# Moving VectorE's and ScalarE's side work around the exponentials in a two-layer kernel on one Trainium2 core

## What is computed

```python
h = gelu(einsum('bnd,hd->bnh', x, fc1_w) + fc1_b)            # 2048 hidden features
shared = einsum('bnh,sh->bns', h, fc2_w) + fc2_b             # 384 features
expert_x = einsum('bnh,bph->bnp', h, experts_w[indices]) + experts_b[indices][:, None, :]
x = x + concatenate([shared, expert_x], -1)
attn_in = tanh(einsum('bsd,da->bsa', x, W1) + b1)
scores = einsum('bsa,a->bs', attn_in, v)
mask = where(pt == 0, l <= j, where(pt == 1, l >= j, l != j))
p = softmax(where(mask, scores[:, None, :], -1e30), -1)
x = x + einsum('bjl,bld->bjd', p, x) / cnt[..., None]
```

## Time and profile before

| | us |
|---|---|
| time, median of 3 runs (1546.91 to 1548.66) | 1547.05 |
| the profiled execution's own time | 1547.54 |
| its span, first to last instruction | 1545.8 |
| TensorE busy | 1448.0 (94%) |
| VectorE busy | 1194.9 (77%) |
| ScalarE busy | 671.7 (43%) |
| mean granted TensorE clock | 0.974 of full speed |

### The profile page before, as it was taken

The page is one execution under the profiler, slowest core; times in us unless marked ns, Lnnn a source line. Parts: engine busy times, 40 slices in busy tenths (PEclk is TensorE's granted clock), DMA queues, the critical chain, the costliest instruction groups (busy, mean ns, idle before and its releaser), DMA issues.

```text
span 1545.8 us, 16174 instructions
## 1 busy us (share of the span) xinstructions
PE 1448.0 (94%) x6488; PEld 663.3 (43%) x6488; DVE 1194.9 (77%) x1749; ACT 671.7 (43%) x889; POOL 0.2 (0%) x4
## 2 busy tenths in 40 slices
PE   6999898999989999899998989999899998989986
PEld 2444343444434444344443434444344443434444
DVE  6867959688595876958689596886958779596885
ACT  4737154361723527145261633517245271542612
POOL 0000000000000000000000000000000000000000
PEclk9999999999999999999999999999999999999998
DMA  5220010201102020010200102010020200100000
GB/s 198 89 82 1 21 62 8 75 1 45 37 14 68 1 80 3 21 62 7 75 1 21 62 14 69 1 55 28 14 68 1 82 0 21 62 7 21 1 28 27
DMA packets 27149, 59.25 MB, mean 38 GB/s; under 512 B 5699, under 2 KB 6083, under 8 KB 24643
## 3 DMA queue, kind: packets, MB, share of 16 engines
q1 hardware_dynamic: 26642, 57.70, 10.8%
q10 hardware_dynamic: 432, 0.53, 0.1%
HBM read 41.45 MB, written 16.78 MB: 38 GB/s over the span
## 4 chain that ended last, share of the span: by engine, by line
PE 58%; DVE 33%; ACT 7%; issue 1%; DVEq 0%
PE pf L279 29%; PE po L325 24%; DVE raw L147 8%; DVE raw L381 7%; DVE hl L153 4%; PE pa L356 4%; DVE xr L147 3%; DVE raw L431 3%; ACT raw L414 3%; DVE mx L197 2%; DVE x L197 2%; ACT L414 1%; ACT hh L156 1%; PE pf L366 1%; ACT g L303 1%
## 5 line engine op out<-in xcount | busy, mean ns | idle before, releaser
L279 PE MATMUL pf<-xh,w1h 128*128 128x512 f16 x1024 | 389.7, 381 | 3.1 <-ACT xh L156 2.1
L279 PE MATMUL pf<-xh,w1l 128*128 128x512 f16 x1024 | 389.1, 380 | 0.4 <-DVE w1l L153 0.4
L279 PE MATMUL pf<-xl,w1h 128*128 128x512 f16 x1024 | 389.2, 380 | 0.1
L325 PE MATMUL po<-hh,w2l 128*128 128x512 f16 x768 | 301.8, 393 | 16.4 <-DVE hl L153 16.4
L325 PE MATMUL po<-hh,w2h 128*128 128x512 f16 x768 | 299.7, 390 | 0.0
L325 PE MATMUL po<-hl,w2h 128*128 128x512 f16 x768 | 299.0, 389 | 0.0
L153 DVE SCALAR_TENSOR_TENSOR hl<-g,ix,hh 128x512 f16<-128x512 f32 x240 | 177.6, 740 | 142.5 <-ACT hh L156 142.0
L303 ACT ACTIVATE g<-pf,b1s,ds 128x512 f32<-128x512 f32 x240 | 185.7, 774 | 148.9 <-PE pf L279 148.7
L381 DVE TENSOR_TENSOR_SCAN raw<-raw 128x512 f32<-128x512 f32 x180 | 212.9, 1211 | 47.6 <-ACT raw L414 47.6
L147 DVE TENSOR_TENSOR raw<-raw 128x512 f32<-128x512 f32 (+1 forms) x315 | 206.5, 683 | 1.0
L156 ACT ACTIVATE hh<-g,ix 128x512 f16<-128x512 f32 x240 | 173.1, 721 | 7.4
(11 more groups left out here) (121 smaller groups left out, 1195.1 us busy)
## 6 DMA issues: line engine op xcount, KB each, us to landing
er<-in_ew SPq DMA_DIRECT2D x16, 1024.0 KB, 4.8
out<-xr SPq DMA_DIRECT2D x64, 256.0 KB, 2.3
xr<-in_xT SPq DMA_DIRECT2D x62, 256.0 KB, 4.1
raw<-in_w SPq DMA_DIRECT2D x16, 256.0 KB, 6.5
er<-in_w SPq DMA_DIRECT2D x3, 1024.0 KB, 10.0
xr<-in_xT ACTq DMA_DIRECT2D x2, 256.0 KB, 5.1
raw<-in_aw SPq DMA_DIRECT2D x1, 256.0 KB, 6.3
ebs<-in_eb SPq DMA_DIRECT2D x16, 0.5 KB, 2.1
```

The costliest lines, as they stand in the source:

```text
L279: return e.matmul(pf[n][:, :], w[:, k, c, :], x[:, c, :], start=c == 0 and i == 0, stop=c == KD - 1 and i == 2)
L325: m = e.matmul(bank[:, :], w, h[:, k, :], start=k == 0 and i == 0, stop=k == NH - 1 and i == 2)
```

## The change

Nothing is computed in another way. TensorE's queue is the same, instruction for instruction. What moves:

- `exps` goes from k = 10 to k = 9, with `finish` before it, and `pool_rest` starts at k = 12.
- `x_biggest(b + 1)` goes from k = 13 to k = 9, the maximum of er from k = 14 to k = 10.
- `split_expert(b, j)` goes from k = 6 to 9 to the second layer's o = 0, one quarter in each j.
- In rows 1 to 14 the four `split_x_high` of the next row go from (0, 3), where they stood together behind `chain_scale`, to (1, 2), (1, 3), (2, 0) and (2, 2), so behind `evacuate(b, 0)`.
- In the last row the four `see` go from k = 10 to 13 to k = 0 to 3, and one of their work tiles takes the other half of er.
- The budgets are 1.75 for each k (1.1 at k = 1), the guessed costs count times 0.92, and the quarters that split the expert count 0.7 of their budget as spent.

```diff
-            credit[0] -= cost * 0.9
+            credit[0] -= cost * 0.92
...
-    same = er[:, 0, 0:S]
+    same = er[:, 1, 0:S]
...
-            if 6 <= k < 10:
-                split_expert(b, k - 6)
-            if k == 13 and not last:
-                x_big = x_biggest(b + 1)
-            if k == 14 and not last:
-                e_big = column(ec(b + 1), er[:, b % 2, :], e_ready[b + 1])
-            if last and 10 <= k < 14:
-                see(b, k - 10)
-            if k == 10:
+            if last and k < 4:
+                see(b, k)
+            if k == 9:
                 finish()
                 exps(b - 1)
+            if k == 9 and not last:
+                x_big = x_biggest(b + 1)
+            if k == 10 and not last:
+                e_big = column(ec(b + 1), er[:, b % 2, :], e_ready[b + 1])
+            if k == 12:
                 pools[0] = pool_rest(b - 1)
-            fill(0.0 if k in (13, 14) else 1.1 if 6 <= k < 10 else 1.85)
+            fill({1: 1.1}.get(k, 1.75))
...
                 if b == 0:
                     first_second_layer(o, j)
+                elif o == 0:
+                    split_expert(b, j)
+                    spent += 0.7
...
-                        x_hi = {c: split_x_high(b + 1, c) for c in range(KD)}
+                        if b == 0:
+                            x_hi = {c: split_x_high(1, c) for c in range(KD)}
                         spent += 0.6
+                    if b and (o, j) in ((1, 2), (1, 3), (2, 0), (2, 2)):
+                        c = ((1, 2), (1, 3), (2, 0), (2, 2)).index((o, j))
+                        x_hi[c] = split_x_high(b + 1, c)
```

## The result

| | kernel before | changed kernel |
|---|---|---|
| median of runs | 1547.86 us (4 runs, 1546.91 to 1549.01) | 1443.26 us (4 runs, 1443.10 to 1443.96) |
| ratio, 95% interval | | 0.9325, 0.9309 to 0.9341 |
| profiled execution, its span | 1547.54, 1545.8 | 1443.96, 1442.1 |

A forecast was written before the change was run, and what follows sets the result against it. TensorE waits for hl and x2l (1.23 + 3.48 us a round) and then runs at low clock (2.2). 96.2 from fourteen rounds, plus 8.0, less 1.4, is 102.8 off the span: 1444.2 us forecast, range 1441 to 1459.

The forecast's parts named there:

- The round without waits: Score to next score in rows 1 to 14 without waits or low clock: 86.6 us, against a mean of 93.47.
- the meeting: TensorE's attention product at output tile 0 and VectorE's x2l arrive within a tenth; 0.1 us of waiting per round taken.
- the walk-through: The change followed instruction by instruction on batch row 8's old clock, putting x2l at 823.3 and the attention product at 823.92.
- two queues at once: Why x2l is late: ScalarE evacuates po0 behind four xh, and VectorE works without a gap; mending one leaves the other.
- The maxima under the exponentials: VectorE's maxima of x and er cost the path nothing while it waits for exponentials; without that cover, 4.85 us.
- The clock: TensorE's low clock behind the long x2l wait, on average 2.2 us a round, goes with the wait.
- Rival B: Small TensorE waits lower the clock too, so 14 x 2.2 = 31 us come back: 1475; chance 0.03.
- The last row: Last batch row's transposes came 6.0 us late, plus 2.2 of clock; new residual about 0.2 late: gain 8.0.
- A: x2l misses TensorE's attention product by 0.5 to 1 us per round: 1450 to 1457; chance 0.09.
- C: Expert's weights land too late for their earlier maximum on VectorE, making it slower: 1561 at 1 us more; chance 0.01.
- D: Something other than these queues holds x2l: 1529 if only the hl wait goes, 1547 if it returns; chance 0.02.
- next in line: Tile 1's attention product could start at 833.9, TensorE there at 835.1; first-layer tile 14's banks keep as much room.

The follow-up runs named there:

- three products: Changed kernel plus three chained, unused 128x512 VectorE operations ahead of the residual of output tile 0: 1474.87 us, ratio 0.9524.
- five products: Changed kernel plus five chained, unused 128x512 VectorE operations ahead of the residual of output tile 0: 1515.43 us, ratio 0.9785.

## Why the prediction was right, point by point

**The sum.** Forecast were 96.2 us from the rounds less 1.4 of remaining waits, and 8.0 from the last row: 102.8 of span. Measured, from the scores of both traces:

| stretch | before | after | gain | forecast |
|---|---|---|---|---|
| to the first score | 117.63 | 118.56 | -0.93 | 0 |
| fourteen rounds | 1308.58 | 1212.53 | 96.05 | 94.8 |
| last row, up to its score | 90.16 | 82.59 | 7.57 | 8.0 |
| behind it | 29.43 | 28.42 | 1.01 | 0 |
| span | 1545.8 | 1442.1 | 103.7 | 102.8 |

The round without waits, 52.70 + 33.87 = 86.57, was right to 0.04. It was taken from one round of before by subtracting two waits and one stretch of low clock, and that is what is left when they are gone. Its halves were less good, and part of the hit is luck: with x2l early (expert's split back) the attention product starts 52.49 behind the score and not 52.70, and from there to the next score it is 34.1 and not 33.87. The first error comes from the due time, which gave the last product ahead of the attention product a whole interval of 0.217, where with x2l early the attention product starts 0.03 behind it (776.32 and 776.35). The low clock's 2.92 were too many by about as much: 865.49 - 828.70 - 34.1 = 2.7. The 1.4 for the meeting were caution: the profile has no wait there, and x2l holds the product by some 0.05 us.

**The meeting.** Scores stood at 771.29 before and 724.79 after, so 46.50 more puts a time of after on the clock of the walk-through:

| | forecast | measured |
|---|---|---|
| maximum of er starts | 790.9 | 744.36 + 46.50 = 790.86 |
| idle time of VectorE before hl of tile 10 | 3.7 | 3.67 |
| hl of tile 11 starts | 798.2 | 751.73 + 46.50 = 798.23 |
| hl of tile 15 starts | 809.6 | 763.01 + 46.50 = 809.51 |
| hl of tile 11 to x2l | 25.10, less 0.12 | 776.60 - 751.73 = 24.87 |
| x2l starts | 823.2 | 776.60 + 46.50 = 823.10 |
| attention product starts | 823.92, due 823.99 | 777.34 + 46.50 = 823.84 |

The sum of some 40 instruction lengths, each from a row of before, missed by 0.1 us. The added products show what that accuracy was needed for: the room is 0.03 us. 0.1 us later, and each round would have been longer by 0.07. The forecast couldn't know this room: x2l came 0.1 earlier than it had and TensorE's own due time was 0.2 earlier, both more than 0.03. That the two errors left no more between them is luck; 0.1 us more would have been 14 x 0.1 = 1.4 in all.

**ScalarE.** The evacuation came 6.8 us ahead of the residual where I had 6. That the xh and VectorE's queue had to be mended together was argued from rows and is now shown from both sides: the xh alone give nothing, and without them 6.7 us of the gain are lost. The first half is shown more sharply than the argument had it. I had called it two queues late at once; VectorE alone held x2l: po0 was evacuated at 824.07 + 0.72 = 824.79, and VectorE came to it at 825.67. None of the 3.32 us of wait came from ScalarE, so the sentence "two queues at once" was wrong, and the one behind it, that mending one alone would leave the other, holds very unequally: mending ScalarE's alone gave nothing, mending VectorE's alone gave all but 6.7 us. ScalarE's queue would have become the limit after the first 0.9 us of gain.

**The maxima under the exponentials.** The step that carries the gain. 4.85 us was the price if the cover went, and 4.81 was measured with the maxima back. Moving the cover instead of the work cost 1.13.

**The clock.** The forecast took 2.2 us of low clock per round as a mean of before and let it go with the wait. It went: the mean granted clock rose from 0.974 to 0.996. Rival B, that any small wait brings it down, is ruled out by waits of 0.86 us in fourteen rounds (exponentials back) and of 1.75 in fourteen (three products), none of which brought it down. The same term was mis-sized in the expectation for five products: 2.2 in each round, measured 1.68 in eleven of fourteen.

**The last row.** 7.57 of the 8.0, so this term was 0.4 too large, and its part for the clock was the one. The transposes started 1482.36 - 1426.21 = 56.15 behind the score before and 1381.33 - 1331.09 = 50.24 now: 5.91, where 6.0 less 0.2 had been put. The rest of the row gained 1.66, where 2.2 had been put for the clock. The window over the low clock in the kernel before, and TensorE's transposes in the changed kernel:

```profile
1482.36:1487.00 4.64, 4.64 (x18) 2.54 (x19) 4.61 (x8) 1.11 (x2) 0.00 (x0) 0.63 0.04 16
```

```profile
1381.33 1.13 PE L500 MATMUL pf<-eye,xr 128*128 128x128 f32 x8
```

A clock of 0.63 over 4.64 us is 1.7 us lost. **Behind the last score** I had nothing, and 1.0 came. Both traces have there the same wait of 7.0 for pl, and low clock behind it. In windows of the changed kernel it is over by 1426, 3.4 us after the wait ends at 1422.64; before, it was at 0.50 up to 1530 and at 0.81 up to 1532, some 5.3 us after the wait's end at 1525.33. Nothing that the change moves lies there. The variants of the changed kernel above took 28.2 us behind their last score (expert's split back) to 29.6 (`pool_rest` back, exponentials back), so before's 29.4 and the 28.4 here both lie in the spread of this stretch. A window of the changed kernel:

```profile
1426.00:1430.00 4.00, 4.00 (x19) 3.26 (x18) 0.76 (x2) 0.00 (x0) 0.00 (x0) 1.00 0.00 0
```

**The start.** 0.93 longer, and nothing was changed there that TensorE waits for. Over the executions profiled here whose batch row 0 is the same, the first score stands between 116.8 and 118.6, so this is within the spread of the start itself. A part of it is clock: behind the wait of 2.28 in batch row 0 it was low in the changed kernel and not in the kernel before. The window of the changed kernel:

```profile
67.00:71.00 4.00, 4.00 (x13) 1.47 (x11) 3.46 (x6) 2.54 (x4) 0.00 (x0) 0.57 0.87 293
```

Of the twelve kernels profiled with this wait two had it, the changed one and the one with the xh alone, and theirs are the two latest first scores, 118.56 and 118.38. The gain in span was thus 0.9 more than forecast, and the median came 0.9 below it.

**Rivals A, C and D** didn't come about: no wait at the meeting, no idle time of VectorE ahead of the maximum of er at 744.36, and the wait for x2l gone with the queues mended. The places named as next in line, tile 1's x2l and the banks of first-layer tile 14, stay without a wait too; the window over the whole round has no idle time of TensorE.

## What to carry to other kernels

When an engine must stand still for something long on another engine, look for work of its own that is needed only later and lay it there; here 4.85 us of maxima in front of work that waited for exponentials of 3.19 us and their two table loads were worth 75 of 105 us, and it cost 1.1 us a round to move the cover a tile away. When two queues meet, mend the one that arrives last first, and mend the other in the same change, because it becomes the limit at once (nothing alone, 6.7 us together). And once the bound engine is full, the time no longer shows what the other queues can spare: read the distance from a common mark to the hand-over (51.81 against 49.90 us here), or add known work until the time moves.

## What the runs showed of the hardware

How often TensorE's granted clock fell behind an idle stretch of it, in the fourteen like rounds of each kernel:

| idle us | where | the clock fell in |
|---|---|---|
| 0.86 | exponentials back, x2l | 0 of 14 |
| 1.07 | before, hl | 0 of 14 |
| 1.75 | three products, x2l | 0 of 14 |
| 1.96 | maxima back, hl | 4 of 14 |
| 2.41 | maxima back, x2l, clock not already low | 3 of 10 |
| 3.21 | five products, x2l | 11 of 14 |
| 3.32 | before, x2l | 14 of 14 |

Outside the like rounds, the wait of 2.28 in batch row 0 was followed by low clock in 2 of 12 kernels, and one of 2.07 in the last row with three added products was too. It isn't a switch at one length: between 2 and 3.2 us of idle time the same wait did and didn't bring it down. Its price where TensorE was the bound: 1.48 us a round with the maxima back (92.90 - 91.42), 1.68 with five products (91.77 - 90.09), and in the kernel before 1.5 to 3.1, from rounds of 92.84 to 94.45 less 86.6 + 4.71 of waits. The Trainium skill ("TensorE: Matmul & The Clock Gate", section "A second HAM failure mode: psum-queue depth-cycling") warns of frequent short pauses between groups of products that keep the clock moving up and down; in these rows pauses up to 1.75 us, once a round, did nothing. Frequent ones weren't run. And where another engine set the pace, a fallen clock was free: 91.42 us with it and without it.

A pair of dependent products on VectorE kept its price after the change. VectorE's timeline in row 8, an independent pair and a dependent one:

```profile
767.71 1.28 DVE L147 TENSOR_TENSOR raw<-raw,xr 128x512 f32<-128x512 f32 x2
...
774.67 1.41 DVE L147 TENSOR_TENSOR xr<-xr,raw 128x511 f32<-128x511 f32 x2
```

The added products show the same where they form a chain: three of them take 2.05 us from start to start and not 3 x 0.60. The prediction gave 0.12 us for the chain that is now split. The Trainium skill ("VectorE: DVE Perf Modes", section "The DRAIN you can't avoid") has such a semaphore cost nothing, as measured there on eight copies. By that rule hl of tile 11 to x2l would be 25.10 us; by the row 24.98; measured 24.87. The 0.12 us between the two is four times the room that was left.
